# Turning x ahead, one wide turn for the Chebyshev sweeps, and transposes for the turns of the first two layers

## The reference

```python
# layer 0: e = x + p * (diag[:, None] * x @ W), W and diag differ for rows below and above 2048
h = adj @ (adj.T @ e);  out = layernorm(h) * gamma + beta + x
# layer 1
out = 1 - 0.1 * x - 0.01 * sum(x * (adj @ x), axis=1, keepdims=True)
# layer 2
h = (adj @ x + x) / deg;  z = concat([x, h]) @ W + b;  out = relu(z) / norm(relu(z))
# layer 3: Chebyshev, K = 4
T1 = L @ x;  T2 = 2 * L @ T1 - x;  T3 = 2 * L @ T2 - T1          # L is adj again
out = x @ w0 + T1 @ w1 + T2 @ w2 + T3 @ w3 + bias
x = layernorm(x + out)                                           # after every layer
```

## Time and profile before

| | us |
|---|---|
| median of 3 runs | 1633.32 (1632.07 to 1633.67) |
| the profiled execution | 1634.46 |
| its span in the trace | 1632.7 |
| PE busy | 1577.2 |
| DVE busy | 564.1 |

### The profile page before, as it was taken

One profiled execution on the slowest core, in us unless ns is written; L12 is line 12 of the kernel. 1 busy time (PEld: TensorE's weight loads), 2 busy tenths in 40 slices (PEclk: granted clock), 3 DMA queues, 4 the chain that ended last, 5 costly groups with the idle time before them and its releaser, 6 DMA issues.

```text
span 1632.7 us, 17981 instructions
## 1 busy us (share of the span) xinstructions
PE 1577.2 (97%) x6938; PEld 762.9 (47%) x6938; DVE 564.1 (35%) x1143; ACT 245.6 (15%) x471; POOL 61.3 (4%) x66
## 2 busy tenths in 40 slices
PE   6799999999999989999999899998999999999998
PEld 4455555555555543334444444444444444444333
DVE  2455555555555565422221433222110010010232
ACT  2233333333333310000000000000000000000000
POOL 0000000000000011100000010000000000000000
PEclk9899999999999999999999999999999999999999
DMA  8689999999999879998688497874288857888896
GB/s 287 270 334 383 392 383 389 387 392 386 388 385 396 338 291 390 421 421 332 241 304 290 148 340 255 299 292 179 104 300 305 296 204 304 296 302 304 320 416 252
DMA packets 118213, 519.02 MB, mean 318 GB/s; under 512 B 15692, under 2 KB 16884, under 8 KB 68084
## 3 DMA queue, kind: packets, MB, share of 16 engines
q1 hardware_dynamic: 102048, 412.66, 68.8%
q10 hardware_dynamic: 16084, 105.23, 15.4%
HBM read 411.69 MB, written 106.17 MB: 317 GB/s over the span
## 4 chain that ended last, share of the span: by engine, by line
issue 99%; POOLq 0%; POOL 0%; DVE 0%
POOL power_out L397 0%; POOLq L395 0%; POOLq L397 0%; DVE rows L797 0%; POOL ident L390 0%; POOLq L392 0%; POOL ident L392 0%; POOLq L992 0%
## 5 line engine op out<-in xcount | busy, mean ns | idle before, releaser
L645 PE MATMUL ps_u<-blk,vectors 128*128 128x512 f32 (+1 forms) x2000 | 743.0, 597 | 4.1 <-DVE part L953 3.2
L645 PEld LDWEIGHTS ps_u<-blk,vectors 128*128 128x128 f32 (+1 forms) x2000 | 294.8, 173 | 401.8 <-issue 399.7
L434 ACT ACTIVATE blk<-ps_turn 128x512 f32<-128x512 f32 x400 | 202.6, 605 | 357.5 <-PE ps_turn L492 357.2
L522 PE MATMUL ps_h<-blk,u_rows 128*64 128x512 f32 x720 | 164.4, 598 | 0.0
L734 DVE TENSOR_REDUCE row_part<-blk 128x4 f32<-128x2048 f32 x68 | 152.3, 2279 | 0.5
L492 PEld LDWEIGHTS ps_turn<-ident,blk 128*128 128x128 f32 x1088 | 120.2, 143 | 22.2 <-issue 21.9
L504 PE MATMUL ps_u<-blk,e 128*64 128x512 f32 x544 | 129.5, 620 | 0.0
L492 PE MATMUL ps_turn<-ident,blk 128*128 128x128 f32 x1088 | 128.2, 276 | 0.0
L718 DVE TENSOR_TENSOR part<-part,ps_h 128x512 f32<-128x512 f32 x80 | 55.0, 687 | 195.8 <-PE ps_h L522 195.8
L953 DVE TENSOR_TENSOR part<-part,ps_u 64x512 f32<-64x512 f32 x28 | 19.2, 685 | 294.2 <-ACT part L447 294.2
L397 POOL TENSOR_TENSOR power_out<-power_in,minus_half 128x4 f32<-128x4 f32 x60 | 60.6, 1010 | 1567.6 <-DVEq L759 1567.6
(11 more groups left out here) (86 smaller groups left out, 625.8 us busy)
## 6 DMA issues: line engine op xcount, KB each, us to landing
blk<-a_transposed SPq DMA_DIRECT2D x291, 1024.0 KB, 5.3
a_transposed<-blk ACTq DMA_DIRECT2D x100, 1024.0 KB, 9.4
blk<-in_adj SPq DMA_DIRECT2D x68, 1024.0 KB, 12.7
nat_far<-in_adj SPq DMA_DIRECT2D x32, 1024.0 KB, 12.9
out<-rows SPq DMA_DIRECT2D x10, 128.0 KB, 3.7
rows<-in_x SPq DMA_DIRECT2D x1, 128.0 KB, 2.3
twice<-in_L_gnn_weight ACTq DMA_DIRECT2D x6, 16.0 KB, 6.1
vec<-in_L_gnn_ln_gamma ACTq DMA_DIRECT2D x1, 32.0 KB, 5.0
```

Source lines behind the costliest of these rows:

```text
L434: nc.scalar.activation(blk[:, n % RING, t, :], ps_t[t][:, :], ACT.Copy)\
L522: mm = pe.matmul(ps_h[n % 2][half(t), :], u_rows[:, t, :], blk[:, n % RING, t, :], start=t < 2, stop=t >= TB - 2)
L645: mm = pe.matmul(acc, left, tiles[:, t, :], start=first, stop=last)
```

## The change

Three things are changed. **First column:** two banks (`ps_h[0]`, `ps_h[1]`) and two copies (`x_turned`, and a piece of `part` that is not yet in use) hold turned x; the product with W goes to `ps_u[1]`; the turn of x for the next pair stands behind each turn_block and the product with W behind each u_part; DVE copies between the two sums and makes e behind them; x is loaded as 8 tiles and 32 tiles instead of 4 and 36, the second piece behind two blocks of adj instead of one. **Chebyshev:** identity and weights stand side by side in `wide` (128 x 128), so that a turn is four products of 128 columns instead of eight of 64; `yw` is interleaved to match. **Layers 0 and 1:** a turn is four plain 128 x 128 transposes, and DVE adds the two halves by a reduction over them.

```diff
+        wide = sb("wide", [P, 2, 2, F])
-        yw = [[ps_t[n][:, k * TB * F:(k + 1) * TB * F].rearrange("p (t f) -> p t f", t=TB) for k in range(2)]
+        yw = [[ps_t[n][:, :].rearrange("p (t k f) -> p t k f", t=TB, k=2)[:, :, k, :] for k in range(2)]
               for n in range(2)]
+        yw_wide = [ps_t[n][:, :].rearrange("p (t g) -> p t g", t=TB) for n in range(2)]
+        y_halves = [ps_t[n][:, :].rearrange("p (t h f) -> p t f h", t=TB, h=2) for n in range(2)]
-        ps_xt_in = ps_h[0]
-        xw_in = ps_h[1][:, 0:TB * F].rearrange("p (t f) -> p t f", t=TB)
+        x_in_turned = [x_turned, part[0:F, 0:BLK]]
+        xw_in = ps_u[1][:, 0:TB * F].rearrange("p (t f) -> p t f", t=TB)
...
-            sp.dma_start(rows[:, 0:TB, :], x_rows[:, 0:TB, :]).then_inc(x_first_loaded, 16)
+            sp.dma_start(rows[:, 0:2 * TB, :], x_rows[:, 0:2 * TB, :]).then_inc(x_first_loaded, 16)
...
-                if n == 0:
-                    sp.dma_start(rows[:, TB:NT, :], x_rows[:, TB:NT, :]).then_inc(x_loaded, 16)
+                if n == 1:
+                    sp.dma_start(rows[:, 2 * TB:NT, :], x_rows[:, 2 * TB:NT, :]).then_inc(x_loaded, 16)
...
             for p in range(COLUMN):
-                turn_block(2 * p)
-                for i in (2 * p + 2, 2 * p + 3):
-                    if i < NB:
-                        turn_x_in(i)
-                    if i % 2 == 0:
-                        turn_block(2 * p + 1)
-                    if i < NB:
-                        times_w(i)
-                u_part(2 * p)
-                u_part(2 * p + 1)
+                for n in (2 * p, 2 * p + 1):
+                    turn_block(n)
+                    if n + 2 < NB:
+                        turn_x_in(n + 2)
+                for n in (2 * p, 2 * p + 1):
+                    u_part(n)
+                    if n + 2 < NB:
+                        times_w(n + 2)
...
-                for k, weights in enumerate(TURN[s]):
+                if s == 1:
                     for t in range(TB):
-                        mm = pe.matmul(yw[n % 2][k][:, t, :], part[:, i * BLK + t * P:i * BLK + (t + 1) * P],
-                                       weights, start=True, stop=True)
+                        mm = pe.transpose(ps_t[n % 2][:, t * P:(t + 1) * P],
+                                          part[:, i * BLK + t * P:i * BLK + (t + 1) * P], ident[:, :])
+                    mm.then_inc(y_back, 1)
+                    return
+                dst = yw_wide[n % 2] if s in (3, 4) else yw[n % 2][0]
+                for t in range(TB):
+                    mm = pe.matmul(dst[:, t, :], part[:, i * BLK + t * P:i * BLK + (t + 1) * P],
+                                   TURN[s], start=True, stop=True)
                 mm.then_inc(y_back, 1)
...
             for p in range(COLUMN):
-                for n in (2 * p, 2 * p + 1):
-                    if n + 2 < NB:
-                        make_e(n + 2)
-                    sum_rows(n)
+                later = [i for i in (2 * p + 2, 2 * p + 3) if i < NB]
+                sum_rows(2 * p)
+                for i in later:
+                    copy_x_in(i)
+                sum_rows(2 * p + 1)
+                for i in later:
+                    make_e(i)
...
                 dve.wait_ge(y_back, n + 1)
-                root = centre(yw[n % 2][0])
+                V.reduce_sum(ta[:, :, :], y_halves[n % 2], AX.X)
                 dve.drain().then_inc(y_used, 1)
+                root = centre(ta)
+                dve.drain()
...
                 dve.wait_ge(y_back, n + 1)
-                V.tensor_tensor(ta[:, :, :], yw[n % 2][0], x_i, ALU.mult)
+                V.reduce_sum(tc[:, :, :], y_halves[n % 2], AX.X)
                 dve.drain().then_inc(y_used, 1)
+                V.tensor_tensor(ta[:, :, :], tc[:, :, :], x_i, ALU.mult)
+                dve.drain()
```

More of the change, by code:

```diff
@@ L418, in _ @@
                 const(twice[half, 0, :], l2_w[F:2 * F, :], weights_loaded)
-                for k in range(1, 4):
-                    const(twice[half, k, :], l3_w[k], weights_loaded)
+                const(twice[half, 1, :], l3_w[3], weights_loaded)
+                for k in range(2):
+                    const(wide[half, k, 1, :], l3_w[k + 1], weights_loaded)
             def store(n):
@@ L481, in times_w @@
                 for t in range(TB):
[L482 to L483 removed]
+                    mm = pe.matmul(xw_in[:, t, :], x_in_turned[i % 2][:, t * P:(t + 1) * P],
+                                   w0[:, int(i >= UB), :], start=True, stop=True)
                 mm.then_inc(xw_ready, 1)
@@ L553, in _ @@
             as_it_is = ident2[:, :]
-            TURN = (None, (as_it_is,), (twice[:, 0, :],), (as_it_is, twice[:, 1, :]),
-                    (as_it_is, twice[:, 2, :]), (twice[:, 3, :],))
+            TURN = (None, as_it_is, twice[:, 0, :], wide[:, 0].rearrange("p k f -> p (k f)"),
+                    wide[:, 1].rearrange("p k f -> p (k f)"), twice[:, 1, :])
             def turn(s, r):
@@ L671, in _ @@
                 for t in range(TB):
-                    mm = pe.matmul(yw[e % 2][0][:, t, :], part[:, i * BLK + t * P:i * BLK + (t + 1) * P], ident2[:, :],
-                                   start=True, stop=True)
+                    mm = pe.transpose(ps_t[e % 2][:, t * P:(t + 1) * P],
+                                      part[:, i * BLK + t * P:i * BLK + (t + 1) * P], ident[:, :])
                 mm.then_inc(y_back, 1)
@@ L707, in make_e @@
                                 diag[:, tiles].unsqueeze(2).broadcast_to([P, TB, F]), ALU.mult)
-                dve.drain()
-                V.tensor_tensor(e_rows[:, tiles, :], rows[:, tiles, :], ta[:, :, :], ALU.add).then_inc(xw_used, 1)
+                dve.drain().then_inc(xw_used, 1)
+                V.tensor_tensor(e_rows[:, tiles, :], rows[:, tiles, :], ta[:, :, :], ALU.add).then_inc(e_ready, 1)
                 dve.drain()
@@ L924, in _ @@
             V.tensor_tensor(w3x[:, 0, :], w3x[:, 0, :], w3x[:, 1, :], ALU.subtract)
-            V.tensor_tensor(twice[:, 1, :], twice[:, 1, :], twice[:, 3, :], ALU.subtract)
+            V.tensor_tensor(wide[:, 0, 1, :], wide[:, 0, 1, :], twice[:, 1, :], ALU.subtract)
+            for k in range(2):
+                V.tensor_copy(wide[:, k, 0, :], ident2[:, :])
             dve.drain()
```

27 lines of the change are left out of this document (17 added, 10 removed).

## The result

The changed kernel took 1577.18 us (median of 4 runs, 1574.93 to 1578.02), beside 1633.49 (4 runs, 1632.07 to 1634.48) for the kernel before on the same chip: a ratio of 0.9655 [0.964, 0.967], 56.3 us less. Forecast were 1580 us and 1567 to 1594.

What follows compares the result with a forecast made beforehand. PE was taken as the bound, busy 1577.2 of 1632.7 us and held in the first column. Savings of 29 + 16.8 + 7.3 = 53.1 us from 1634.5 gave 1581.4, the median 1.1 lower: 1580 us, range 1567 to 1594.

Steps and rivals of the forecast that it cites:

- Pairs 1 to 3 of the first column: First column: each pair falls from 16.9 to 10.3 us at the full clock, DVE keeping up; 19.8 us saved.
- rival (3): First column: transposes standing together let the clock fall, 3.2 us lost in each of four pairs: 1593 us; chance 0.05.
- Start and pair 0: Kernel's start: block 0 is turned while x's second piece loads, so pair 1 starts at 26.5; 10.4 us saved.
- The 1.2 us set aside for DMA: First column: taken off the gain because the loads' lead is still being built in the first pairs; upper bound 4.5 us.
- rival (2): DMA holds the first column and the first sweep: 1588 to 1591 us; chance 0.08.
- a slack of 19 us: Loads of blocks: landing 13.2 us after issue, with a slot back every 32 us, they have nearly 19 us to spare.
- Rival (6): Slower: blocks come late in every later column; 45 pairs at 1.2 us more each would cancel the gain; chance 0.02.
- Chebyshev: 16.8 forecast: Chebyshev sweeps: a turn falls from 1.93 to 1.09 us of PE, 0.84 saved in each of 20; 16.8 us.
- Layers 0 and 1: 7.3 forecast: Turns there: PE saves 0.48 us in 17, three lose 0.3 to DVE's 0.77 us reduction and drain; 7.3 us saved.
- My check for them: Layers 0 and 1: the sign to look for was PE's waits at the first turns growing by 0.3 us.
- rival (4): DVE becomes the bound in layers 0 and 1, its 0.77 us paid in all 20 ends: 1603 us; chance 0.04.
- Rival (5): The first column doesn't change, because a pair still waits for DVE: 1600 us; chance 0.03.

Runs made afterwards that it cites:

- later weights: The changed kernel with ACT's sixteen loads of small weights issued one after each copied block from block 3 on: 1575.67 us, ratio 0.9661 to the kernel before.
- the column alone: The kernel before with only the first column's new order, banks and loads of x, all turns as before: 1601.25 us, ratio 0.9812.
- the kernel with mixed turns: The changed kernel with layer 0's first turn and layer 1's first and last as products, without the reduction: 1573.90 us, ratio 0.9644 to the kernel before.
- the doubled reduction: The changed kernel with DVE's new reduction done twice in each of the 20 ends of layers 0 and 1: 1580.57 us, ratio 0.9675 to the kernel before.

## Why the prediction was right, and where its terms were off

The forecast mechanism happened, at 1577.18 us for 1580. That the total came so near is partly luck: the first column fell short of its term by 2.1 us, and the clock in the sweeps, which the sum had at nothing, gave 10.2. The span's 60.1 us, against the 53.1 of the sum, come apart as follows.

**Pairs 1 to 3 of the first column** were forecast at 10.3 us each and lasted 10.31; they brought 20.0 us where 19.8 was forecast. DVE kept up, with the first scaling's product done at 38.0, 1.3 us before the second times_w at 39.32, where 0.9 was left. The clock read 1.00 from 26 to 60 us, so rival (3) is refuted: from 30.04 to 34.55 us PE did nothing but transposes, 3.6 us of blocks and 0.9 of x, and the u_part behind them still took 1.94 us, its time at the full clock. By the Trainium skill ("TensorE: Matmul & The Clock Gate", section "Part 4: PE-mode transpose") a transpose doesn't count as busy time for the full clock in the way a product does; for the float32 transposes here this trace, like the earlier trace rows, speaks against that.

**Start and pair 0: 10.4 forecast, 6.9 measured**, the step that failed. Pair 1 was to start at 26.5 and started at 30.04. I had costed PE, DMA and the clock, and not ACT, whose loads of weights stood ahead of its first copy; with block 0 turned 5.7 us earlier, ACT became late for it. The later weights moved pair 1 forward by 4.9 us, more than the 3.5 that were missing, so this cause is shown. The 1.2 us set aside for DMA were not needed while ACT held the column up; without that hold PE waited for a load. Together the first column brought 26.9 us by pair 5 where 29 was forecast.

**DMA, rival (2).** It did not decide, but part of it was there: with ACT out of the way block 9 came late by 2.23 us, and a slack of 19 us did not exist in the first pairs. By the slack that I took from a later column it should have been impossible; in the first column the loads' lead is 7 to 12 us. In the first sweep the loads, at the same 421 GB/s as before, now land when they are used, with PE waiting 0.56 us in one place: the small cost that was named beside the sum. Rival (6) didn't occur: pairs in later columns kept their length, and the 26.9 us stood unchanged to the last of them.

**Chebyshev: 16.8 forecast, 17.8 measured** (0.89 in each of 20 turns, read as steps in PE's lead). A wide turn costs 1.09, as the row from which I took it, only at the edges of a sweep. In the middle rows, 12 of the 20, it takes 0.89 us (1134.70 - 1133.81) where the old one took 1.73 (1177.20 - 1175.47). Where turns follow one another they are cheap too, 1110.89 - 1108.91 = 1.98 us for two, against 3.71 for two of the old ones (in the column alone, at the full clock, 1114.31 to 1118.02), 0.87 saved in each:

```profile
1133.81 1.05 PE L582 MATMUL ps_turn<-wide,part 128*128 128x128 f32 x8
1134.70 5.75 PE L656 MATMUL ps_u<-blk,vectors 128*128 128x512 f32 x13
```

**Layers 0 and 1: 7.3 forecast.** In the same place four transposes take 0.58 us and the product turn 1.03 (the kernel with mixed turns), so a turn saves 0.45 and not 0.48. The three waits grew by 0.74, 0.40 and 0.48 us, and a fourth of 0.37 appeared at 699.98, which the prediction didn't name. My check for them was misstated: 0.3 is what the wait and the shorter turn come to together (0.74 - 0.45), not what the wait itself grows by. The sum of it, 20 x 0.45 less 1.6 for the three waits, 0.4 for the fourth and 0.6 for the late load, is 6.4. The reduction took its 0.69. DVE's waits for turns in layer 0 fell from 31.3 to 18.6 us, as forecast, so rival (4) fell with the doubled reduction. What is left of the span for this term after the others, 60.1 - 26.9 - 17.8 - 10.2, is 5.2 us. PE's lead says nearly the same: it grows from 26.9 to 37.4 us over both layers, of which about 5 is low-clock stretches. Alone this part gave 8.0 with the clock taken out by the estimate above. The forecast lies between, and closer than this it isn't settled.

**The term that was missing: the clock in the sweeps.** The prediction put the low-clock stretches of the sweeps at the lower end of the range and at nothing in the sum. Before, they stood at 595.3, 725.0, 1148.3 and 1346.3 us (6.8 us each) and at 936.7 and 1134.6 (3.4 each), 34 us in all; after, at 569.5, 883.6, 900.6 and 1098.6, 3.4 each, 13.6 in all. At half the clock a stretch loses half of its length where PE is busy, so 17 against 6.8: 10.2 us. These made good the first column's 2.1 us and more. Part of it is not earned by what was changed in those places, since the column alone gained nearly 9 us in unchanged sweeps. The prediction's remark that a stretch follows each longer run of turns doesn't hold: behind both runs of turns in sweeps 3 and 4 the column alone has none. What sets off a stretch is shown only this far: it follows a longer wait of PE or a run of turns, and the same code can have it or not. Which rule decides stays open, and with it why the parts don't add up to better than 2 us.

Rival (5) is refuted by the first column, and the median of 1577.18 lies inside the range.

## What to carry to other kernels

When PE's start is moved forward, look at every engine that hands something to it in the first microseconds, with all that stands ahead in its own queue: here ACT's list of small loads took a third of the gain forecast at the start, and behind it stood DMA. A slack read in a steady stretch doesn't hold for the ramp. An addition to DVE is free only where PE doesn't wait for DVE; use the cheap form in the many turns and look at each of the few where PE waits: the old form won 0.3 us in two of them and nothing in the third.

Don't expect parts to add up, and don't credit an edit with all that its kernel gains: compare the mean granted clocks first, take (1 - clock) x span as a bound on what they can explain and not as its price, look in the traces for the stretches that differ, and repeat runs when the rest is some us.

## What the runs showed of the hardware

The granted clock was worth some 22 of the 60.1 us (23.3 by the mean clocks): 11.9 in the first column, where four stretches of 6.8 us became one of 3.4, part of its 26.9, and 10.2 in the sweeps. One program's runs differed by 9 us in step with it. DMA of this one core moved 412 GB/s over 34 us of loads and stores mixed. Products of 64 columns and of 128 columns, with 128 rows of fp32 as the stationary operand, cost nearly the same: eight instructions in 0.97 and in 1.09 us at the edges of a sweep, in 0.87 and in 0.89 in its middle rows, so a turn pays by the number of products. And ACT took 0.36 to 0.65 us to issue each small load, 9.5 us for sixteen with nothing else done, and 1.28 us for its table before it could copy at all.
